# Cross-attention keys and values of two pairs made in the first stage, a causal mask on quarters of the array, expert rows cleared ahead, and a router on unscaled tokens

## The chip, the cores and the metric

One core of one Trainium2 chip. The metric is device microseconds from the start of the program to its end. Three timed runs of the kernel before and one profiled execution are at hand.

## The reference

The input x is 16 tiles of 128 tokens by 256 features in float32, the context likewise. Four blocks run one after another:

1. `q = layernorm(x)`, `x = x + q + tril(C C^T) q` per tile, where C is the tile's context.
2. With `h = layernorm(x)`: a latent attention of 16 heads of 8 features (RMS norm, a projection to 128, rotated queries and keys, causal softmax, projection up), whose result is added to h to give r. Then eight experts of 512 hidden features: `t = rmsnorm(r) * g2`, softmax over `t @ router_w`, the two best experts' `silu(t w1) * (t w3) @ w2`, weighted by their two probabilities normed to 1. `x = x + r + y`.
3. Cross attention of 16 heads of 64 features: queries from a layer norm of x, keys and values `C @ w_kv`, which depend on the context alone. `x = x + tanh(gate) * (out @ w_out + b_out)`.
4. `t = layernorm(x)`, 16 experts of 256 hidden features, the two best by `t @ router_w` with sigmoid weights, and a shared expert of 512. All added to x.

## The kernel before

**Order of work.** Nothing is scheduled at run time. `latent_phases`, `expert_phases`, `cross_phases`, `shared_phases` and `last_phases` (L165 to L380) list phases: an engine, an estimated duration in ns, what the phase comes after, the PSUM banks that it fills and a due time. `Plan.order` (L108) simulates the engines and always takes the phase with the smallest start plus due time; `LEAD` (L76) moves the due time of all phases of a name. What comes out is one fixed order for each engine's queue (TensorE, VectorE, ScalarE, GpSimd and SP, which issues DMAs), and an engine stands still at a phase whose semaphores aren't there yet, whatever is behind it.

**First stage, 16 batches b of one tile each.** `ctx`/`q1` (L668, L679) make block 1; `hnT`, `c`, `qkv` project; GpSimd's `rope_p` (L1756) and VectorE's `rope` rotate; `qkT` transposes queries and keys; `qkh`/`qkl` split them in a high and a low part, and GpSimd's `kmh`/`kml` (L1771) spread the keys over four masked copies, by `masked` (L639). `s(b)` (L713) first writes the causal mask into four banks of 512 columns with four bf16 products of the identity and `negb` (L718), then waits for `kmh` and `kml` and adds three products on groups of 32 array rows (L727). `max`, `exp`, `pT` (L731, transposes at L737), `pT_e` (L1048, a copy out of PSUM at L1052), `pv` (L740, 64 matmuls at L751), `onrm` and `wup` follow; `r` (L1340) makes the residual tile r. Then comes a chain: `sq` (L1054) squares on ScalarE, `eps3` on VectorE, `pow3` on GpSimd, and `tt` (L1358) on VectorE writes `r * rstd * g2` to a token tile TT. `tT` (L761) transposes TT (L765, L766), `log` makes the router's logits, `ra` and `rb` (L1367, L1389) the choice and the row that each token gets, and `sc` (L1789) on GpSimd scatters the token to its expert's rows in the DRAM tensor `xs_dram` (8 or 16 experts of 2176 rows of 259 floats).

**Between first stage and experts.** `route` (L1408) makes the list TI of tiles (expert and first row), 39 at most. An expert's last tile is only partly filled, so `pad_sp` (L1855) and `pad_act` (L1067) write 128 zero rows behind each expert's last, four experts on SP's queue and four on ScalarE's. `xs(0, 0)` (L1866) waits for the list, all scatters, all pads and `latent_over`, reads the row from TI and loads the first 128 rows. `xT` first issues `FILL[0]` = 40 matmuls (`keep_busy`, L784), which compute nothing that is used. `wa`, `wv` copy the expert's weights; `gate_up` (L800, matmuls at L812), `down` (L816, three matmuls on high and low parts by `mm3`, L661 to L665) and `y` do a tile.

**Cross attention, 8 pairs jj of two tiles.** For a pair TensorE makes keys in four units `K(jj, u, half)` (L827, 12 matmuls of 256 columns each, by `mm3`), values in four units `V(jj, u, i)` (L840, 6 of 512 columns), queries `Q` likewise, then `S`, `T`, `PV`, `W`. Keys lie in a ring of three tiles, values in one of seven. `ch`/`cl` split a pair's context, `kw`/`vw` and `kwl`/`vwl` the weights. Blocks of the shared expert (`SG`, `SD`) are spread over the end of this stage and of the last one. `pad_sp(1)` clears the second experts' rows ahead of `xs(1, 0)`.

**Loads.** `loads` (L1843) issues on SP, with no wait: x tiles 0 to 3 (0.5 MB), constants (0.3), context tiles 0 to 3 (0.5), small weights (0.6), x tiles 4 to 15, context tiles 4 to 15 (1.6), the first experts' gate and up weights (8.4 MB) and down weights (4.2).

## Time and profile before

| | us |
|---|---|
| three timed runs | 995.28, 1000.51, 1004.29 |
| median | 1000.51 |
| profiled execution, whole | 990.24 |
| its span | 988.4 |
| mean granted TensorE clock in it | 0.981 |

The profile is of one execution. Its times are from the start of the span. PE is TensorE's matmuls, PEld its weight loads, DVE VectorE, ACT ScalarE, POOL GpSimd, SP SyncE; L12 is line 12 of the kernel. A row of a timeline has start, duration, engine, line, operation, output and inputs, count, and in brackets an idle time before it and what ended it. Matmuls are pipelined, so durations of neighbours overlap; the distance between starts is what one costs.

### The profile page before, as it was taken

The numbers are of one execution on the slowest core, as the hardware profiler recorded it, in microseconds if no ns is written. First come the engines' busy times: TensorE is split into PE (matmuls) and PEld (weight loads), VectorE is DVE, ScalarE is ACT, GpSimd is POOL, SyncE is SP. The second block draws the span as 40 slices with busy tenths as digits, with TensorE's granted clock in tenths as the row PEclk, the third lists the DMA queues.
The fourth block names the chain that finished last, engine by engine and source line by source line (L and its number), as shares of the span: only waits on it lengthen the run. The fifth ranks groups of instructions, "written<-read, shape, count | busy, mean of one in ns | idle before, by whom it ended". The sixth has DMA issues, their size and how long they took to land.

```text
span 988.4 us, 24441 instructions
## 1 busy us (share of the span) xinstructions
PE 911.9 (92%) x8250; PEld 815.2 (82%) x8250; DVE 720.7 (73%) x1957; ACT 609.8 (62%) x1690; POOL 289.3 (29%) x371
## 2 busy tenths in 40 slices
PE   5798888879999999978999999999998999999997
PEld 3566666547999999977988999989887979999986
DVE  6877788664766667666898887566686736888857
ACT  1378777734666666655776686575877425767640
POOL 3747767640000000005645432202011202333320
PEclk9999999979999999988999999999999999999999
DMA  9700000012411111113101010000040872333325
GB/s 378 341 13 18 29 34 24 27 45 78 144 50 54 50 54 49 49 31 125 39 28 55 24 33 23 23 2 23 1 172 22 333 218 72 93 91 98 93 93 212
DMA packets 37323, 82.57 MB, mean 84 GB/s; under 512 B 5489, under 2 KB 28785, under 8 KB 35921
## 3 DMA queue, kind: packets, MB, share of 16 engines
q1 hardware_dynamic: 29760, 61.63, 17.9%
q0 software_dynamic: 6864, 18.85, 5.7%
q8 instruction: 68, 1.11, 0.5%
q10 hardware_dynamic: 576, 0.53, 0.2%
q14 instruction: 55, 0.44, 0.2%
HBM read 55.95 MB, written 25.04 MB: 82 GB/s over the span
## 4 chain that ended last, share of the span: by engine, by line
PE 62%; issue 13%; DVE 9%; POOL 6%; DMA 4%; ACT 3%; SPq 3%; ACTq 0%; DVEq 0%; POOLq 0%
PE ps L812 15%; PE ps L663 9%; PE ps L665 8%; PE ps L664 8%; POOL yt_dram L1820 4%; PE ps L876 4%; PE ps L897 3%; PE ps L886 3%; DVE BIG L1328 2%; PE ps L737 2%; PE ps L727 1%; PE ps L718 1%; DMA CT<-in_ctxT 1%; SPq L1864 1%; PE ps L955 1%
## 5 line engine op out<-in xcount | busy, mean ns | idle before, releaser
L663 PE MATMUL ps<-BIGR 128*128 128x256 f32 (+1 forms) x826 | 258.6, 313 | 12.5 <-DVE CTR L1576 4.7
L812 PE MATMUL ps<-BIG 128*128 128x128 f32 x2000 | 253.0, 276 | 5.9 <-DVE BIG L1556 4.9
L812 PEld LDWEIGHTS ps<-BIG 128*128 128x128 f32 x2000 | 238.5, 193 | 8.2 <-DVE BIG L1556 6.8
L665 PE MATMUL ps<-BIGR 128*128 128x256 f32 x762 | 216.3, 284 | 0.0
L663 PEld LDWEIGHTS ps<-BIGR 128*128 128x128 f32 x826 | 158.4, 192 | 20.2 <-issue 10.4
L664 PE MATMUL ps<-BIGR 128*128 128x256 f32 (+1 forms) x570 | 168.6, 296 | 0.0
L665 PEld LDWEIGHTS ps<-BIGR 128*128 128x128 f32 x762 | 145.7, 191 | 0.0
L1098 ACT COPY BIG<-BIG 128x512 f32 (+1 forms) x86 | 70.0, 814 | 99.4 <-PE ps L812 93.6
L664 PEld LDWEIGHTS ps<-BIGR 128*128 128x128 f32 x570 | 109.1, 191 | 1.8
L1549 DVE TENSOR_TENSOR BIGR<-BIG,BIGR 128x512 fp32r<-128x512 f32 (+1 forms) x86 | 80.3, 934 | 36.4 <-ACT BIGR L1107 36.2
L1812 POOL DMA_INDIRECT BIG<-ys_dram,YI x32 | 36.2, 1131 | 231.5 <-DMA ys_dram<-BIG 223.7
L1192 ACT ACTIVATE BIG<-ps,sm 128x128 f32<-128x128 f32 x256 | 91.6, 387 | 14.8 <-DVE sm L1650 14.6
L1799 POOL DMA_INDIRECT xs_dram<-TT,PI x64 | 65.9, 1030 | 82.3 <-DVE PI L1406 71.3
L1820 POOL DMA_INDIRECT yt_dram<-BIG,IX x47 | 47.7, 1016 | 127.8 <-DVE BIG L1569 124.9
L1045 ACT ACTIVATE BIG<-ps,BIG 128x128 f32<-128x128 f32 x256 | 72.5, 409 | 9.9 <-DVE BIG L1328 9.9
L1734 POOL TENSOR_TENSOR st<-st,CS 128x1 f32<-128x1 f32 (+1 forms) x48 | 31.0, 647 | 160.8 <-DVE st L1277 160.6
L664 PE MATMUL ps<-CTR,BIGR 128*128 128x256 f32 x256 | 73.2, 286 | 0.0
L1556 DVE TENSOR_TENSOR BIG<-ps,BIG 128x256 f32<-128x256 f32 (+1 forms) x86 | 46.7, 543 | 36.2 <-PE ps L812 36.2
L1107 ACT CAST BIGR<-BIG 128x512 fp32r (+1 forms) x86 | 69.4, 807 | 5.4 <-PE ps L665 5.4
L1647 DVE TENSOR_REDUCE sm<-ps 128x4 f32<-128x512 f32 x64 | 44.0, 687 | 25.8 <-PE ps L876 25.6
L1192 ACT ACTIVATION_READ_ACCUMULATOR BIG<-ps,sm 128x1 f32 x256 | 57.5, 225 | 0.0
L1542 DVE COPY BIG<-BIG 128x512 f32 (+1 forms) x86 | 47.2, 549 | 7.8 <-issue 4.0
(224 smaller groups left out, 1905.0 us busy)
## 6 DMA issues: line engine op xcount, KB each, us to landing
BIG<-in_wd SPq DMA_DIRECT2D x2, 4096.0 KB, 35.3
BIG<-in_wgu SPq DMA_DIRECT2D x1, 6144.0 KB, 19.2
BIG<-xs_dram SPq DMA_DIRECT2D x47, 129.5 KB
BIG<-xs_dram SPq DMA_DIRECT2D x39, 128.0 KB
ys_dram<-BIG SPq DMA_DIRECT2D x39, 128.0 KB, 1.7
BIG<-yt_dram SPq DMA_DIRECT2D x16, 256.0 KB, 5.7
xs_dram<-zero SPq DMA_DIRECT2D x20, 129.5 KB, 6.8
X<-in_x SPq DMA_DIRECT2D x4, 512.0 KB, 7.7
```

The lines of the kernel that those rows point to most:

```text
L663: pe.matmul(o, l[0], r[0], start=start, stop=False)
L664: pe.matmul(o, l[0], r[1], start=False, stop=False)
L665: return pe.matmul(o, l[1], r[0], start=False, stop=stop)
L812: i = pe.matmul(o[:, c * 128:(c + 1) * 128], wt[:, at:at + 128], x[:, k * 128:(k + 1) * 128], start=k == 0, stop=k == 1)
L1045: i = act.activation(p_[g][:, at], ps("s", b, i=g)[:, at], ACT.Exp, bias=sm[:, 4 * g + n:4 * g + n + 1])
L1098: act.copy(W_[r][j % 2][:, n:2 * n], WGU[:, bass.ds(e * (2 * n) + n, n)]).then_inc(S["gu_upper"], 1)
L1107: act.copy(D_[j % len(D_)][:, 0:n], WD[:, bass.ds(e * n, n)]).then_inc(S["down_hi"], 1)
L1192: i = act.activation(xp_[s % 4][:, at], ps("S", s // 2, i=s % 2)[:, at], ACT.Exp, bias=sm[:, 4 + n:5 + n], accum_out=sm[:, 8 + n:9 + n])
L1542: v.tensor_copy(W_[r_][j % 2][:, 0:n], WGU[:, bass.ds(e * (2 * n), n)]).then_inc(S["gu_lower"], 1)
L1549: v.tensor_tensor(wd[:, n:2 * n], WD[:, bass.ds(e * n, n)], wd[:, 0:n].bitcast(F32), ALU.subtract).then_inc(S["down_lo"], 1)
L1799: pool.indirect_dma_start(XS, bass.IndirectOffsetOnAxis(ap=PI[:, b, k:k + 1], axis=0), TT[tile_of(r, b)][:, :], None).then_inc(sem(f"scatt ...
L1820: pool.indirect_dma_start(YT, bass.IndirectOffsetOnAxis(ap=IX[:, j % 4:j % 4 + 1], axis=0), Y_[1][j % 3], None).then_inc(sem(f"results_pla ...
```

## The change

1. **Keys and values of pairs 4 and 6** (`EARLY_KV`). The 2.1 MB of `wkv` and the two pairs' contexts are loaded at once after the first four loads (`wkv_in`), ahead of the rest of x and context (`rest_in`). `kvw` on ScalarE and `kvwl` on GpSimd split the weights in four parts, `ctxh`/`ctxl` the contexts. 16 units `kv(m)` on TensorE, of the same matmuls as K and V before, fill a bank of the first stage; `kv_e` copies it to one of four tiles and `kv_s` stores that (0.26 MB) to DRAM. In cross attention `kl` and `vl` load them back in place of the K, V, `K_e` and `V_e` phases of these pairs. The expert weights' region is used for this, so they are loaded in parts: down weights behind `kmh(3)`, a quarter of the gate and up weights behind the four `kvwl`, the other 6.3 MB (`load_w0b`) when all 16 stores have landed.
2. **Mask.** `causal(b)` replaces the four products of 128 by 128 by eight on quarters of 64 by 64 (four of 512 and four of 256 columns), placed between the first and the second of the three products; the first no longer waits for `kml`.
3. **Router.** `tT` transposes r itself instead of TT, the router's weights are scaled by g2 once, the logits' difference is multiplied by rstd in `gates_a`. `r(b)` also waits for `tT(b-2)`.
4. **Rows cleared ahead.** `pad_act` and `pad_sp(0)` go. Seven groups of two and one of three blocks of 128 rows of all eight experts are cleared by SP during the first stage (`blank`), each scatter of batch 2g waits for group g. `xs` reads TI before its waits.
5. `FILL[0]` is 30 instead of 40. `LEAD` has other values throughout, and a new table `NUDGE` moves single phases by up to 4.6 us of due time; so the orders of all engines differ.

```diff
-FILL = (40, 24)
+BLANK = [range(2 * g, 2 * g + 2) for g in range(7)] + [range(14, 17)]
+EARLY_KV = (4, 6)
+FILL = (30, 24)
...
+        due += LEAD.get(...) + NUDGE.get(key, 0)
...
+    p.add("SP", 60, ("wkv_in",), ("loads",), late=12000)
+    p.add("SP", 200, ("rest_in",), ("wkv_in",), late=17000)
+    for g in range(len(BLANK)):
+        p.add("SP", 120, ("blank", g), ("tt", 2 * g - 2) if g else ("kmh", 0), late=4000)
+    p.add("SP", 60, ("wd_in",), ("rest_in",), ("kmh", 3), late=12000)
-        add("PE", 220, ("tT", b), ("tt", b), banks=[(misc, ("tT_e", b))])
+        add("PE", 220, ("tT", b), ("r", b), ("log", b - 2), banks=[(misc, ("tT_e", b))])
+    for u in range(4):
+        p.add("ACT", 950, ("kvw", u), ("setup_a",), ("wkv_in",))
+        p.add("POOL", 2050, ("kvwl", u), ("kvw", u))
+    p.add("SP", 60, ("load_w0a",), ("kvwl", 3), ("kmh", 3), late=12000)
+    for j in range(len(EARLY_KV)):
...
+        for m in range(8 * j, 8 * j + 8):
+            add("PE", 1440, ("kv", m), ("ctxl", j), ("kvwl", ...), ("kv_s", m - 4), banks=[("misc", ("kv_e", m))])
+            add("ACT", 466, ("kv_e", m), ("kv", m), ("kv_s", m - 4))
+            add("SP", 60, ("kv_s", m), ("kv_e", m), late=2000)
+    p.add("SP", 60, ("load_w0b",), ("kv_s", 8 * len(EARLY_KV) - 1), ("load_w0a",), late=18000)
...
                 for x, y in ((0, 0), (0, 1), (1, 0)):
+                    if y:
+                        causal(b)
+                        pe.wait_ge(*done("kml", b))
...
+            def causal(b):
+                for n in range(2):
+                    for half in range(2):
+                        for rows in range(2):
+                            g, at = 2 * (rows ^ half) + n, slice(64 * rows, 64 * rows + 64)
+                            lo = 64 * half
+                            m = (negb if rows == half else negx)[at, lo:128].rearrange("p (o t) -> p o t", o=1)
+                            o = ps("s", b, i=g)[64 * half:64 * half + 64, :].rearrange(...)[:, :, lo:128]
+                            pe.matmul(o, identb[at, at], m.broadcast_to([64, 4, 128 - lo]), start=False, stop=False)
...
             def tT(b):
-                pe.wait_ge(*done("tt", b))
-                tt = TT[tile_of(0, b)]
+                pe.wait_ge(*emptied("wup", b))
+                t = r_[b % 2]
...
+            def kv_e(m):
+                act.wait_ge(*full("kv", m))
+                if m >= 4:
+                    act.wait_ge(sem(f"kv_stored{m % 4}"), 16 * (m // 4))
+                act.copy(kvs_[m % 4], ps("kv", m)[:, :]).then_inc(*frees("kv", m))
...
+            def blank(g):
+                if g:
+                    sp.wait_ge(*done("tt", 2 * g - 2))
...
+                for c in BLANK[g]:
+                    sp.dma_start(XS[0:E0 * CAP, 0:D].rearrange("(e c) n -> c e n", c=CAP)[128 * c:128 * c + 128],
+                                 zero[:, 0:D]...broadcast_to([128, E0, D])).then_inc(sem(f"cleared{g % 3}"), 16)
...
             def xs(r, j):
                 if j == 0:
                     sp.wait_ge(sem("tiles_listed"), r + 1)
+                at = sp.value_load(TI[j:j + 1, 1:2], ...)
+                if j == 0:
                     for i in range(3):
                         sp.wait_ge(sem(f"scattered{i}"), ...)
-                    sp.wait_ge(sem("padded_sp"), 16 * (E1 * r + E0 // 2))
-                    sp.wait_ge(sem("padded_act"), 16 * (E0 // 2))
+                    if r:
+                        sp.wait_ge(sem("padded"), 16 * E1)
...
+            def load_w0b():
+                for i in range(4):
+                    sp.wait_ge(sem(f"kv_stored{i}"), 16 * len(range(i, 8 * len(EARLY_KV), 4)))
+                sp.dma_start(big(0, 48 * KB), a["wgu0"][:, 0:48 * KB]).then_inc(sem("wgu_loaded"), 16)
```

## Rows read from the trace of the kernel before

**Rows 1.** The page's first part: busy us, share of the span, instructions.
```profile
PE 911.9 (92%) x8250; PEld 815.2 (82%) x8250; DVE 720.7 (73%) x1957; ACT 609.8 (62%) x1690; POOL 289.3 (29%) x371
```

**Rows 2.** Stretches: length; busy PE, PEld, DVE, ACT, POOL; clock; DMA; GB/s.
```profile
0.00:46.00 46.00, 26.92 (x138) 18.96 (x138) 34.57 (x135) 12.21 (x45) 26.29 (x55) 0.96 0.94 386
46.00:212.00 166.00, 145.08 (x1820) 105.14 (x1820) 129.13 (x389) 125.62 (x425) 105.04 (x151) 0.98 0.07 24
...
232.00:435.00 203.00, 202.60 (x1771) 202.63 (x1772) 135.51 (x188) 128.34 (x191) 0.00 (x0) 0.99 0.20 60
...
450.00:600.00 150.00, 146.06 (x1277) 131.37 (x1276) 127.25 (x373) 103.27 (x350) 69.10 (x74) 0.99 0.12 37
600.00:757.00 157.00, 153.62 (x1443) 138.94 (x1441) 106.54 (x336) 113.78 (x399) 25.10 (x27) 1.00 0.11 40
757.00:813.00 56.00, 53.86 (x396) 49.18 (x391) 32.16 (x103) 19.01 (x30) 7.15 (x8) 1.00 0.69 244
```

**Rows 3.** TensorE's timeline in cross attention, 461.9 to 467.6 us.
```profile
461.89 0.28 PE L663 MATMUL ps<-BIGR 128*128 128x256 f32 x1
...
464.77 0.40 PE L663 MATMUL ps<-BIGR 128*128 128x512 f32 x1
...
467.34 0.39 PE L665 MATMUL ps<-BIGR,CTR 128*128 128x512 f32 x1
```

**Rows 4.** TensorE's timeline in the first stage, 103 to 115 us.
```profile
103.31 0.97 PE L727 MATMUL ps<-BIGR 32*128 32x512 f32 x12
...
111.93 0.17 PE L781 MATMUL ps<-mb,strictb 128*128 128x8 bf16 x1 [0.88 <-DVE mb L1387]
...
113.02 1.03 PE L718 MATMUL ps<-negb,identb 128*128 128x512 bf16 x4
113.98 0.98 PE L727 MATMUL ps<-BIGR 32*128 32x512 f32 x12
114.89 1.95 PE L751 MATMUL ps<-BIG 128*32 128x128 f32 x64
```

**Rows 5.** Groups by line in 50 to 205 us: busy, mean ns, idle before.
```profile
L765 PE MATMUL ps<-CS,TT 128*128 128x128 f32 x14 | 4.2, 302 | 4.5 <-DVE TT L1361 4.4
...
L1052 ACT COPY BIG<-ps 128x512 f32<-128x512 f32 x60 | 36.8, 623 | 7.3 <-PE ps L737 6.5
...
L641 POOL TENSOR_TENSOR BIGR<-BIGR,CS 128x512 fp32r<-128x512 f32 x26 | 26.8, 1042 | 10.5 <-ACT BIGR L1036 10.4
```

**Rows 6.** Timeline of all engines between the first stage and the experts.
```profile
212.00 0.48 DVE L1346 SCALAR_TENSOR_TENSOR BIG<-BIG,st,ps 128x256 f32<-128x256 f32 x1 [0.85 <-PE ps L759]
...
214.96 0.45 PE L765 MATMUL ps<-CS,TT 128*128 128x128 f32 x1 [1.36 <-DVE TT L1361]
...
218.26 11.26 PE L787 MATMUL ps<-negb,identb 128*128 128x512 bf16 x40
...
220.79 0.96 POOL L1799 DMA_INDIRECT xs_dram<-TT,PI  x1 [0.31 <-issue]
...
223.82 0.15 DVE L1469 CAST TI<-sc 128x1 int32<-128x1 f32 x1
...
226.56 1.04 ACT L1107 CAST BIGR<-BIG 128x1024 fp32r x1
...
229.35 3.71 SPq L1882 DMA_DIRECT2D BIG<-xs_dram  x4
...
232.40 2.74 PE L812 MATMUL ps<-BIG 128*128 128x128 f32 x16 [0.51 <-issue]
```

**Rows 7.** DMA queues in 220 to 229 us, issues in 60 to 200 us.
```profile
q10 hardware_dynamic: 576, 0.53, 23.2%
...
xs_dram<-TT,PI POOLq DMA_INDIRECT x26, 2.7
```

**Rows 8.** The chain that ended last: two waits for DMAs (start, length).
```profile
4.42 12.19 DMA CT<-in_ctxT
...
224.25 4.06 DMA xs_dram<-zero
```

More of the change, by code:

```diff
@@ L28 @@
 VPAD = 88
-FILL = (40, 24)
+EARLY_KV = (4, 6)
+LAST_KV = max(j for j in range(NB // 2) if j not in EARLY_KV)
+FILL = (30, 24)
 KB = 256
@@ L100, in add @@
         name = (engine, key[0], key[1] if key[0] in BY_STAGE else 0)
[L101 removed]
+        due += LEAD.get(key[0] + str(key[1]) if key[0] in BY_STAGE else key[0], 0) + NUDGE.get(key, 0)
         if name in self.latest:
@@ L253, in expert_phases, with ctx_before @@
             add("SP", 60, "ys", ("y", r, j), late=2000)
+def ctx_before(j):
+    return max((i for i in range(j % 2, j, 2) if i not in EARLY_KV), default=-1)
 def cross_phases(p):
@@ L869, in scores @@
                 if i == 0:
-                    pe.wait_ge(*emptied("K", jj, u, 1))
+                    if jj in EARLY_KV:
+                        n = 2 * jj + u
+                        pe.wait_ge(sem(f"keys_back{n % 3}"), 16 * len([x for x in range(n % 3, n + 1, 3) if x // 2 in EARLY_KV]))
+                    else:
+                        pe.wait_ge(*emptied("K", jj, u, 1))
                     pe.wait_ge(*emptied("Q", jj, u, 1))
@@ L892, in PV @@
                 pe.wait_ge(*emptied("T", 2 * h + 1))
-                pe.wait_ge(*emptied("V", jj, u, i))
+                if jj in EARLY_KV:
+                    pe.wait_ge(sem(f"values_back{h % 7}"), 16 * len([x for x in range(h % 7, h + 1, 7) if x // 4 in EARLY_KV]))
+                else:
+                    pe.wait_ge(*emptied("V", jj, u, i))
                 v = xv_[h % 7]
@@ L1000, in setup @@
                 act.copy(negb[:, :], cst["neg"]).then_inc(sem("constants_cast"), 1)
+                for x in range(2):
+                    act.copy(negx[64 * x:64 * x + 64, :], cst["neg"][64 - 64 * x:128 - 64 * x, :]).then_inc(sem("constants_cast"), 1)
                 act.wait_ge(sem("small0_loaded"), 16)
@@ L1004, in setup @@
                 act.mul(wqkv[:, 0:128], wqkv[:, 0:128], SC0).then_inc(sem("w_down_scaled"), 1)
+                for k in range(2):
+                    act.mul(rt0[:, k, :], rt0[:, k, :], g2c[:, k:k + 1]).then_inc(sem("router_scaled"), 1)
             def hnT_e(b):
@@ L1790, in sc @@
                 pool.wait_ge(*done("rb", r, b))
-                if r == 0 and b == 0:
-                    pool.wait_ge(sem("zeroed"), 6)
+                if r == 0:
+                    pool.wait_ge(*done("tt", b))
+                    if b == 0:
+                        pool.wait_ge(sem("zeroed"), 7)
+                    for g in range(len(BLANK)):
+                        if BLANK[g][0] == b:
+                            pool.wait_ge(sem(f"cleared{g % 3}"), 16 * sum(len(BLANK[k]) for k in range(g % 3, g + 1, 3)))
                 if r and b == 0:
```

297 lines of the change are left out of this document (219 added, 78 removed), and 78 rows, old and new, of tables (LEAD, NUDGE).

## The prediction

> **What bounds the kernel now.** I read the engines' busy shares first. TensorE is busy 92% of the span, VectorE 73%, ScalarE 62%, GpSimd 29% [rows 1], so I asked where its idle 76.5 us lie. The table by stretches answers that [rows 2]. In the experts' first pass (232 to 435 us) TensorE is idle 0.4 of 203 us; in cross attention (450 to 757) 7.3 of 307; up to 813 another 2.1 of 56. Work taken from there comes off the time nearly one for one. The first stage (0 to 212) is different: 19.1 us idle in its first 46, then 20.9 of 166, while VectorE and ScalarE are busy 129 and 126 us of those 166. A batch takes 10.67 us there (103.31 to 113.98, products of batch to batch [rows 4]), and TensorE's own work 87% of that: it is the bound here as well, but with holes, 0.88 us in front of the count at 111.93 for instance [rows 4]. Then comes a tail without much matmul: from the last residual (212.00) to the first expert's gate product (232.40) there are 20.4 us [rows 6].
>
> The sum is made against the profiled execution: 988.4 us of span and 1.8 us around it, 990.2. The three timed runs have a median of 1000.5, which is 10.3 more; I take the same 10.3 for the kernel after.
>
> **Keys and values of pairs 4 and 6.** They leave cross attention and are made in the first stage. A K unit is 12 matmuls of 256 columns: two units run from 461.89 to 464.77, so 1.44 us each. A V unit is 6 of 512 columns: two from 464.77 to about 467.57, 1.40 each [rows 3]. A pair has 4 and 4: 11.4 us, and two pairs 22.7 us. TensorE gives this up where it is 98% busy. I take 21.0: VectorE is the next engine there, busy 106.5 of the 157 us of 600 to 757, which hold some four pairs (307 us for 8, 38.4 each), so 26 us a pair, while TensorE is left with 27 in pair 4 or 6 [rows 2]. It is close, and rings of three key tiles let neighbours even it out, so only 1.7 us are left behind. The bounds are 12 us (VectorE rules in both pairs) and 22.7. The four loads of keys and eight of values that replace the units go over SP, which has almost nothing else there, each a ring slot ahead of its use; they cost nothing unless SP stands at a wait for something later.
>
> **The same work in the first stage** adds 22.7 us to TensorE. ScalarE gets 16 copies like the 623 ns ones [rows 5] (10.0), four roundings of 1024 weight columns (1.04 us each by the nearest row, at 226.56 [rows 6]) and two context ones, 15 us in all; VectorE 1.4 us. GpSimd gets four subtractions of 1024 columns, twice the 512 of its 1042 ns row [rows 5]: 8.3 us, and they come in the first 46 us, where it is busy 26.3 [rows 2]. They can delay the first batches by up to 5 us, but these are the very holes in which the new matmuls lie. How much of 22.7 is hidden? Nothing at least; at most 15, half of the 19 us idle at the start and a third of the 21 later, since most of those later holes are shorter than a unit of 1.4 us. The weights can't be ready before some 20 us: with what is queued in front of them they are 4.5 MB, 12 us at the 386 GB/s of the first 46 us [rows 2], and rounding and subtraction follow. So I take 7.0, nearer the low end. The two later loads of the context and X move behind the new weights; batch 4 waits for the context until 16.6 us already [rows 8], and I count a shift of 2 us inside the same 7.0.
>
> **Mask.** Four matmuls of 512 columns lie from 113.02 to 113.98, 0.96 us [rows 4]. Now eight act on quarters of 64 by 64: four of 512 and four of 256 columns. If the quarters run side by side this is two of 512, 0.43 us; one after another it is 6 of 512, 1.28. The nearest rows are the products on 32 rows of the array: 12 of 512 columns in 0.91 us (113.98 to 114.89), against 4 whole ones in 0.96 [rows 4]. Those pack, so I take side by side. Twelve such products would be 0.64 us if four run together without loss, and they take 0.91: entering a packing has a price of 0.1 to 0.25. I take 0.66 for the mask, a gain of 0.30 a batch and 4.8 us in 16 batches; bounds 8 gained and 5 lost. The Trainium skill (TensorEngine Tiling (Array Packing), Key Properties) says that changing the tiling mode drains the array; after this edit the mode changes twice more in each batch. The 0.27 us that the 12 products take over 0.64 agree with a cost of that kind; no run here yet shows it alone. By the page's other rule, tiles that run independently, the gain without drains would be 8 us.
>
> **Router on unscaled tokens.** The transposes no longer wait for the square sum, the power and the scaling: 14 pairs of them start right after the scaling and wait 4.5 us on it [rows 5]. I take 2.5, since the next thing in TensorE's order then waits for its own input. At the end it counts whole: the last transposes start at 214.96 and could at 212.62, 0.14 behind the end of the residual (212.00 + 0.48): 2.3 us [rows 6].
>
> **Rows cleared ahead.** Between the tile list (223.82 + 0.15) and the first row load (229.35) stand eight DMAs of zeros, which land at 228.31 [rows 6, 8]. They go; what is late next is the last scatter (issued from 220.79 on, 2.3 earlier by the router's step, landing 2.7 later [rows 6, 7]) and the tile list at about 221.6. A load issued at 222.5 gives a gate product 3.05 later (229.35 to 232.40), at 225.5: 6.9 us sooner, of which 2.3 are the router's. I round both to 7.0. The filling matmuls, 30 instead of 40, at 0.28 each (11.26/40 [rows 6]) end at about 224.3 and don't hold it up. In exchange 17 blocks of 8 x 128 rows of 1 KB are cleared under the first stage: 17,408 packets. The pads of ScalarE's queue took 23.2% of 16 engines' time over 9 us (220 to 229) for 576 packets, 58 ns each [rows 7], so 17,408 take 63 us of the DMAs in a stage that uses 7% of them [rows 2]. A group of two blocks holds SP's queue 7.4 us, every 21.3 us. The first experts' weights now come late: 6.3 MB, 16.3 us at 386 GB/s, issued when the last K/V store has landed; needed at 222, so they are hidden if the last unit is made before 200.
>
> **Sum.** Cross attention -21.0; first stage +22.7 - 4.8 - 2.5 - 7.0 = +8.4; tail -7.0. Together -19.6. The reordered queues elsewhere (the table of leads) I count as 0, bounds 4 either way. 990.2 - 19.6 = 970.6, as a median of runs 980.9: **981 us**.
>
> **Rivals.**
> A. The first stage absorbs nothing, and GpSimd's 8.3 us delay its start by 4: +7.0 + 4.0, 992. For it: GpSimd and VectorE are both busy in 17 to 46 us. Against: TensorE's 19 idle us there. Chance 0.12.
> B. Better packing: 14 us absorbed and the whole 22.7 in cross attention: 8.7 less, 972. For it: K/V units depend on nothing of a batch and can stand in any hole. Chance 0.20.
> C. VectorE or the rings rule in pairs 4 and 6; only 12 of 22.7 come back: 990. For it: 26 against 27 us above. Chance 0.10.
> D. The clearing paces the first stage: the scatter of batch 2g waits for group g, issued two batches before, and K/V stores and the late weights stand behind it in SP's queue. The price is the packet's time: a group fits its 21.3 us up to 166 ns a packet, 2.9 times the 58. At 225 ns a group takes 28.8, 7.5 too long; over 7 intervals 52.5 us, less the slack of one group (21): +31, 1012, slower. Against it only the 58 ns, measured on 129 KB pieces in another stretch. Chance 0.08. On order the Trainium skill (DMA: Bandwidth & Descriptors, HWDGE ordering) says that one issuing engine's descriptors are taken in ring order on each DMA engine. By that a K/V store waits out at most one group; no run here shows it. By rows that is 7.4 us, and with four store tiles a copy waits only if units follow closer than about 2 us.
>
> **Numbers.** Forecast 0.50 (974 to 988), B 0.20, A 0.12, C 0.10, D 0.08. A median moves by about 1% without a cause, so 990.5 is the border of faster. Faster: the forecast, B, and most of C, 0.80. Same: A and the rest of C, 0.12. Slower, over 1010.5: D, 0.08. The range leaves out half of B and D: 968 to 996.
>
> **What would show it.** Right: experts' first gate product between 230 and 238; nine or ten K/V units before 100 us; a mask step of 0.6 to 0.7 us between its neighbours; row load within 1 us of the tile list; cross attention (first K to last W) 19 to 22 us shorter with TensorE still over 97%. Wrong: batches over 11.5 us apart, ScalarE waiting for stores or VectorE for scatters (D), a mask step over 0.96, a wait for the experts' weights behind the tile list, or VectorE over 95% busy in pairs 4 and 6 (C).

## The result, and the profile after

Over 20 runs each the kernel after takes 992.3 us in the median (986.5 to 997.5), the kernel before 999.7 (993.1 to 1004.5). The ratio is 0.9931 [0.9912, 0.9951]: 7.3 us less in the medians, where 19.6 were forecast. On two more chips it was 0.9943 [0.9908, 0.9978] and 0.9982 [0.9946, 1.0017]. The profiled executions say the opposite, 990.2 before and 996.3 after, because single executions differ by 10 us and chips by 15 (medians of before from 985 to 1000). So the sizes below come from ratios, and the profiles only say where the time lies. Both kernels were profiled again with the experiments (c2_before, c1_after and c4_after below). The first row is a start in us from the start of the span, the others are the lengths of the stages behind it:

```
                              before  before   after   after   after
                              first   again    first   again   third
last residual of first stage  212.0   218.8    227.2   225.7   218.7
  to first gate product        20.4    21.4     22.1    23.6    23.8
first experts                 210.1   209.2    209.2   209.7   209.5
cross attention, to the
  second gate product         374.9   377.3    352.9   353.2   352.9
second experts                135.1   130.5    145.5   138.0   139.8
rest                           35.9    35.7     37.6    37.6    37.6
```

(Experts: first gate product to last result copy in the first, to last gate product in the second.) Cross attention gives 22 to 24 us, as forecast. But the tail behind the last residual is 2 us longer instead of 7 shorter, and the second experts, whose arithmetic the change doesn't touch, take 8 us more in the mean (141.1 against 132.8).

The page's busy times of after, which answer to [rows 1]:

```profile
PE 909.2 (91%) x8304; PEld 810.8 (82%) x8304; DVE 724.2 (73%) x1957; ACT 610.3 (61%) x1694; POOL 294.7 (30%) x375
```

TensorE's work is 2.7 us less than before, its idle time 9 us more. The stretches of after, columns as in [rows 2]: first stage, tail, first experts, cross attention from the first scores to the last output, and on to the second gate product:

```profile
46.00:227.00 181.00, 160.47 (x1999) 117.34 (x1997) 136.63 (x422) 132.12 (x443) 114.75 (x170) 0.98 0.53 158
227.00:249.00 22.00, 11.01 (x42) 4.96 (x42) 10.95 (x49) 4.17 (x8) 5.20 (x6) 0.68 0.84 328
249.00:452.00 203.00, 202.71 (x1774) 202.69 (x1775) 136.61 (x192) 128.36 (x191) 0.00 (x0) 0.99 0.20 61
483.00:759.00 276.00, 264.20 (x2504) 236.24 (x2503) 227.33 (x694) 193.76 (x713) 85.85 (x95) 1.00 0.17 55
759.00:811.00 52.00, 51.28 (x356) 46.14 (x355) 27.44 (x91) 15.61 (x25) 4.67 (x5) 1.00 0.73 262
```

The second row is the tail: TensorE half idle, the DMA engines 84% busy, where the forecast had a nearly silent tail. What they move stands on SP's queue (start, time of the group, tile, count) and in the chain:

```profile
205.43 3.67 SPq L2180 DMA_DIRECT2D kv_dram<-BIG  x2
209.15 2.73 SPq L2123 DMA_DIRECT2D xs_dram<-zero  x3
213.22 3.71 SPq L2180 DMA_DIRECT2D kv_dram<-BIG  x2
226.57 0.33 SPq L2186 DMA_DIRECT2D BIG<-in_wgu  x1
245.94 7.42 SPq L2154 DMA_DIRECT2D BIG<-xs_dram  x5
```
```profile
233.65 12.11 DMA xs_dram<-TT,PI
245.94 2.10 DMA BIG<-xs_dram
```

in the landing of the weights' load (source L2186), and in the waits of 226 to 252 us:

```profile
DMA to landing us min/median/max: 18.4/18.4/18.4
```

```profile
ACT BIG L1308 <- DMA BIG<-in_wgu: 13.6, 1, 13.6
PE ps L984 <- DMA BIG<-xs_dram: 8.6, 1, 8.6
```

The tile list is ready at 236.4, as forecast about 9 us behind the last residual; the row load is issued at 245.94. In between it waits for the last scatter, which lands after 12.11 us, at 245.8, instead of after 2.7 [rows 7]. The 6.3 MB of first-expert weights run at the same time: issued at 226.57, because the last stores of keys and values, issued from 213 to 217, land only then, and landed 18.4 us later, at 245.0. ScalarE's copy of the first expert's weights (L1308) waits 13.6 us for them and ends at 247.0. So the gate product of 249.3 stands behind both, and a last scatter that landed sooner would by itself have won about 2 us (an estimate from these two times). The ScalarE copies of the 16 units show when these were made:

```profile
L1357 ACT COPY BIG<-ps x16: 567/598/740, 22.9 to 214.1; 128x512 f32<-128x512 f32 x16
```

Eight of them are done by 46 us, hidden in the start; the other eight come only from 164 us on, at the end of the plan. The forecast had written "hidden if the last unit is made before 200".

### The profile page after: what moved, and what is told of

Its sections match the earlier page's. It is cut to its first block, busy times and chain, and to the rows that moved or that the text cites. A ratio compares the mean times of both kernels' runs of the same rounds, so it can differ in the third digit from the quotient of the medians.

```text
span 994.5 us, 24561 instructions
## 1 busy us (share of the span) xinstructions
PE 909.2 (91%) x8304; PEld 810.8 (82%) x8304; DVE 724.2 (73%) x1957; ACT 610.3 (61%) x1694; POOL 294.7 (30%) x375
## 3 DMA queue, kind: packets, MB, share of 16 engines
q8 instruction: 68, 1.11, 0.5%
## 4 chain that ended last, share of the span: by engine, by line
PE 55%; issue 15%; DVE 14%; POOL 5%; ACT 5%; DMA 4%; another core or an unknown queue 0%; SPq 0%; DVEq 0%; POOLq 0%; ACTq 0%
PE ps L999 15%; PE ps L833 7%; PE ps L835 7%; PE ps L834 7%; POOL yt_dram L2066 4%; ACT BIG L1262 3%; PE ps L1086 2%; PE ps L1110 2%; PE ps L1096 2%; PE ps L921 2%; PE ps L897 2%; PE ps L1168 2%; DVE BIG L1884 1%; PE ps L935 1%; DMA xs_dram<-TT,PI 1%
## 5 line engine op out<-in xcount | busy, mean ns | idle before, releaser
L833 PE MATMUL ps<-BIGR 128*128 128x256 f32 (+1 forms) x826 | 260.4, 315 | 12.2 <-DVE BIGR L1807 3.3
L835 PE MATMUL ps<-BIGR 128*128 128x256 f32 x778 | 223.1, 287 | 0.0
L834 PE MATMUL ps<-BIGR 128*128 128x256 f32 (+1 forms) x602 | 179.0, 297 | 0.0
L833 PEld LDWEIGHTS ps<-BIGR 128*128 128x128 f32 x826 | 159.1, 193 | 20.3 <-issue 14.2
L835 PEld LDWEIGHTS ps<-BIGR 128*128 128x128 f32 x778 | 149.2, 192 | 0.7
L1308 ACT COPY BIG<-BIG 128x512 f32 (+1 forms) x86 | 70.1, 815 | 108.5 <-PE ps L999 70.0
L834 PEld LDWEIGHTS ps<-BIGR 128*128 128x128 f32 x602 | 116.3, 193 | 1.8
L1420 ACT ACTIVATE BIG<-ps,BIG 128x128 f32<-128x128 f32 x256 | 91.2, 384 | 15.6 <-DVE BIG L1887 12.8
L2066 POOL DMA_INDIRECT yt_dram<-BIG,IX x47 | 45.6, 971 | 143.0 <-DVE BIG L1800 140.3
L1262 ACT ACTIVATE BIG<-ps,BIG 128x128 f32<-128x128 f32 x256 | 72.6, 394 | 3.1 <-DVE BIG L1557 2.5
L834 PE MATMUL ps<-CTR,BIGR 128*128 128x256 f32 x224 | 63.6, 284 | 0.0
L1335 ACT CAST BIGR<-BIG 128x256 fp32r<-128x256 f32 (+1 forms) x86 | 43.0, 500 | 23.5 <-DVE BIG L1787 22.1
L1420 ACT ACTIVATION_READ_ACCUMULATOR BIG<-ps,BIG 128x1 f32 x256 | 56.8, 222 | 0.0
L1773 DVE COPY BIG<-BIG 128x512 f32 (+1 forms) x86 | 46.8, 544 | 13.5 <-issue 11.2
## 6 DMA issues: line engine op xcount, KB each, us to landing
BIG<-xs_dram SPq DMA_DIRECT2D x47, 129.5 KB
```

Of the source, the lines that this page charges most:

```text
L833: pe.matmul(o, l[0], r[0], start=start, stop=False)
L834: pe.matmul(o, l[0], r[1], start=False, stop=False)
L835: return pe.matmul(o, l[1], r[0], start=False, stop=stop)
L1262: i = act.activation(p_[g][:, at], ps("s", b, i=g)[:, at], ACT.Exp, bias=sm[:, 4 * g + n:4 * g + n + 1])
L1308: act.copy(W_[r][j % 2][:, n:2 * n], WGU[:, bass.ds(e * (2 * n) + n, n)]).then_inc(S["gu_upper"], 1)
L1420: i = act.activation(xp_[s % 4][:, at], ps("S", s // 2, i=s % 2)[:, at], ACT.Exp, bias=sm[:, 4 + n:5 + n], accum_out=sm[:, 8 + n:9 + n])
```

## The experiments

Labels c1 to c5 are five chips; all runs of one number share a chip and its runs of before. "Control" is the kernel after on the same chip; c2, c3 and c5 have none. A figure in brackets behind a ratio is its 95% interval.

**Repeats.** Both kernels again, for the table above.

> The changed kernel again, unchanged, for a second profile beside the first and a second ratio. If the profile of after is typical of it: last r about 227, first gate product of the first experts 20 to 23 us behind it, last wx about 759, and the second experts (first gate product to last) about 145 us. If the 10.4 us that the second experts took longer than in before were chance, this profile has them near 135 instead. Ratio 0.990 to 0.996.

Measured: 0.9943 [0.9908, 0.9978].

> The kernel before again, for a second profile. If the first profile was typical: last r at 212, first gate product at 232, last wx at 769, the second experts about 135 us. Its first profile (990.2 us) lies below all 20 timed runs, so I expect some stage to be 5 to 10 us longer here, most likely one with many waits for DMAs.

Measured: 0.9996 [0.9963, 1.0028]. The stage that differed was the first, by 6.8 us in the last residual; it is spread over the batches, of which some take 12.0 instead of 10.7 us. The second experts came out shorter, not longer.

> After unchanged, as the control on this chip: last r to first gate product 22 to 24 us, second experts 135 to 146 us, ratio 0.992 to 0.996.

Measured: 0.9982 [0.9946, 1.0017].

**The late units.** Orders of three engines edited behind the planner, the eight late units all made before 182 us; the banks of their outputs chosen anew:

```diff
+MOVED = [("PE", ("kv", 15), ("pT1", 11)), ..., ("ACT", ("kv_e", 15), ("exp0", 12)), ...,
+         ("SP", ("kv_s", 15), ("load_w0b",)), ("SP", ("load_w0b",), ("blank", 6)),
...
+    for engine, key, ahead_of in MOVED:
+        orders[engine].insert(orders[engine].index(ahead_of), key)
```

> Units 8 to 15 of the early keys and values moved from batches 9 to 13 to batches 1 to 9 in the orders of TensorE, ScalarE and SP; nothing else. Theory T1, the last stores hold back the load of the 6.3 MB of expert weights, and this load shares the rings with the last scatters: the load is issued before 205 instead of at 226.6 and has landed before the first row load, the last scatter lands in under 6 us instead of 12.1, and the first gate product follows the last r by 13 to 16 us instead of 22.1; the total falls by 3 to 8 us against after (some of it given back because the first stage packs worse, r 15 up to 5 us later), ratio to before 0.983 to 0.990. Rival T2, the weights were ready about when the rows were anyway and the tail is the chain over the last batch: the distance from r 15 to the gate product stays over 20 us and the total does not fall, ratio 0.993 or above. Rival T4, the loss is all in the first stage, which cannot hide the units wherever they stand: as T2, with r 15 at 227 or later.

Measured: 0.9894 [0.9817, 0.9971], 4 runs. The weights were issued at 183.9, the tail fell to 14.0 us; the control had 23.6. But the last residual came at 235.2 instead of 225.7, so the first gate product stood at 249.2 as before. T1 is right about the tail, and its gain was lost again in front of it. Of the 9.5 us, 4.6 are there by the residual of batch 12 (199.8 against 195.1), over the batches that took the units in. For the rest, the stretches of c1_kv_sooner show one cause:

```profile
190.00:195.00 5.00, 4.99 (x92) 3.43 (x84) 2.11 (x4) 3.80 (x14) 4.05 (x4) 1.00 1.03 436
195.00:200.00 5.00, 3.00 (x12) 1.92 (x12) 2.84 (x9) 2.81 (x10) 2.19 (x4) 0.69 1.02 363
200.00:205.00 5.00, 4.32 (x26) 2.13 (x27) 2.14 (x9) 0.93 (x5) 0.73 (x1) 0.50 0.79 244
205.00:210.00 5.00, 4.45 (x64) 3.85 (x66) 3.24 (x10) 4.33 (x15) 2.08 (x2) 0.50 0.92 220
```

The third figure from the right is the granted clock. With no units left there TensorE stood idle for 1.4 us ahead of 188.5 and for 1.7 ahead of 196.7, and the clock went from 1.00 to 0.50, from 2.4 to 1.2 GHz, until about 210. (A second one has no name: ScalarE waits 6.7 us, until 232.5, for something that the profile doesn't tell.) The next experiment puts fill products there:

```diff
                 vacant(pe, *key)
+                keep_busy(ps(*key), {(1, 12): 5, (3, 13): 6, (1, 13): 6}.get((g, b), 0))
```

> The kernel with units 8 to 15 moved ahead, with 17 fill products (0.21 us each at full clock) on TensorE at the three places of batches 12 and 13 where it waited 1.4 to 1.7 us for ScalarE or VectorE. Its first stage was 9.5 us longer than that of after, of which 4.7 behind r 12, where no unit is left, and the granted clock was 0.50 to 0.69 from 195 to 210. Theory: the units at the end of the stage kept TensorE busy enough for the full clock; with fill in their place the clock is 0.94 or above in 195 to 210, r 15 comes 3 to 6 us sooner (229 to 232) and the first gate product at 243 to 246 instead of 249.2. Rival: the clock does not fall for idle time in this place, or r 12 to r 15 is set by the expert weights loading at that time beside the scatters: r 15 stays at 235.

Measured: 0.9895 [0.9858, 0.9931]; last residual at 225.5, gate product at 238.9. Beside a control:

> The units moved ahead with fill at the three idle places, again, beside the control on one chip. From the pairs so far (0.9895 against 0.9931 to 0.9943): 3 to 5 us below the control in the median; first gate product 8 to 10 us sooner in the profile. If the total falls by as much as the gate product is sooner, 8 us or more; if less, the rest goes into the second experts again, which took 144.8 in its first profile.

Measured: 0.9906 [0.9864, 0.9947], median 975.5 against 983.6 of the control. Gate product 240.1 against 242.5, second experts 137.1 against 139.8. The same stretches of c4_sooner_fill:

```profile
195.00:200.00 5.00, 4.29 (x35) 2.06 (x34) 2.80 (x10) 2.42 (x10) 1.81 (x4) 1.00 0.79 251
200.00:205.00 5.00, 4.27 (x80) 3.46 (x80) 4.45 (x18) 4.67 (x16) 2.06 (x3) 1.00 1.09 283
205.00:210.00 5.00, 3.23 (x30) 1.78 (x30) 2.88 (x6) 2.59 (x9) 3.54 (x5) 1.00 0.98 234
```

Seventeen products that compute nothing kept the clock at 1.00, with the DMA engines as full as without, and the step from residual 12 to 13 is 11.2 us instead of 14.7 (the controls have 11.6 and 12.1). The tail is 13.9 us instead of 23.8, but the last residual comes 7.5 us later than in the control, and this lateness (8.2 us) is there by the residual of batch 12: units at the end of the stage are hidden better than units in its middle, and what the early load wins in the tail is mostly paid for with that. The two spans differ by 8.8 us: 2.4 up to the first gate product, which is what the edit did, 3.7 from there to the second, 2.7 in the second experts. The last two parts I can't put down to the edit.

**The load in two.**

```diff
             def load_w0b():
+                sp.wait_ge(*full("kv", 8 * len(EARLY_KV) - 1))
+                sp.dma_start(big(0, 32 * KB), ...)
                 for i in range(4):
                     sp.wait_ge(sem(f"kv_stored{i}"), ...)
-                sp.dma_start(big(0, 48 * KB), ...)
+                sp.dma_start(big(32, 16 * KB), ...)
```

> After with the 6.3 MB load in two: 4.2 MB as soon as the last unit of keys and values is made (no wait for its stores), 2.1 MB behind the stores. If the wait for the stores is what costs: first part issued at 216 to 217 instead of 226.5, gate product 3 to 6 us sooner. If the rings are full anyway until 224 with the clearing writes, the bytes only queue up sooner: gate product sooner by under 2 us, and the last scatters land later than in after. I hold the second likelier.

Measured: 0.9923 [0.9885, 0.9961], tail 20.9 us. The first part was issued at 208.4, 11 us ahead of the second, and the second landed at 236.3, 16.8 us behind its own issue, with the last scatter at 237.3. The ratio can't be told from that of after (0.9931). A wait less was worth at most 3 us of tail here, while the rings (the DMA engines' queues) were full: the clearing writes, the first part and the scatters share them.

**The clearing writes.** One batch sooner (and the last two groups each ahead of a store in SP's order), then all of them early:

```diff
-                    sp.wait_ge(*done("tt", 2 * g - 2))
+                    sp.wait_ge(*done("tt", max(2 * g - 3, 0)))
```

> The clearing writes of groups 1 to 7 are paced one batch earlier (wait for tt 2g-3 instead of 2g-2), and in SP's order group 6 stands ahead of the store of unit 9 and group 7 ahead of that of unit 12. Theory T3, the last stores of keys and values queue behind the three writes of group 7 (issued at 209.15) and land late, and the weights with them: the load of the weights is issued by 221 instead of 226.6, the first gate product comes 3 to 6 us sooner after r 15, ratio 0.988 to 0.991. T1 without this queueing (the stores are late because the units are made late): under 2 us. Rival D of the prediction, clearing itself slows the stage: no change either, since as much is written.

Measured: 1.0003 [0.9965, 1.0041]. It did not test what it was made for: the last group was issued at 206.90 instead of 208.13, since the scaling it now waited for is done only then. It is somewhat slower than the control for a reason that I did not find.

```diff
+CLEAR = [range(0, 2), range(2, 6), range(6, 17)]
-                    sp.wait_ge(*done("tt", 2 * g - 2))
+                    sp.wait_ge(*done("tt", g - 1))
-                for c in BLANK[g]:
+                for c in CLEAR[g]:
```

> After with the same 17 clearing writes in three groups instead of eight (2, 4 and 11 blocks, paced by tt 0 and tt 1, in SP's order where groups 0 to 2 stood), so that the last ends near 140 us and none stands behind 180. Theory: in after the three writes of the last group (issued at 209, 3.1 MB) keep the rings at 250 GB/s and full until about 224, the last two stores of keys and values and the last scatters land behind them, and the load of the expert weights can start only at 226.5. Then here: the load is issued at 216 to 219, the row load at 236 to 240 instead of 246, the first gate product 5 to 10 us sooner than the 249.3 of both profiles of after, ratio 0.984 to 0.989. Rival, the same bytes written in a burst from 85 to 135 us delay the scatters there and with them the rows of three batches: the first stage to r 8 grows by 3 us or more and eats it. Rival, the load of 6.3 MB alone sets the tail: gate product sooner by less than 3 us.

Measured: 1.0113 [1.0050, 1.0176], slower than before. The rings between 80 and 140 us, the scatters in that stretch, and a wait of GpSimd in 151 to 175:

```profile
80.00:140.00 60.00, 50.30 (x643) 36.55 (x642) 47.68 (x155) 43.86 (x151) 40.52 (x62) 1.00 1.08 275
```
```profile
xs_dram<-TT,PI POOLq DMA_INDIRECT x10, 8.8
```
```profile
POOL xs_dram L2048 <- DMA xs_dram<-zero: 12.1, 1, 12.1
```

The scatters landed after 8.8 us in the median instead of 2.7, one waited 12.1 us for the clearing of its rows, and one batch took 21.1 us (8 to 9, against 11.8 to 13.4 in the profiles of after). This is the mechanism of rival D, at a place where I had put it myself.

> Both edits on after: clearing early and the load in two. Rings are free from 216 on: first part issued at 216, all weights landed by 234 to 236, gate product at 237 to 242 (after: 249.3), total 8 to 12 us below after, ratio 0.981 to 0.986. If the tail is not set by these loads: as after, 0.993.

Measured: 1.0018 [0.9986, 1.0050], the same stall. The tail is 17.0 us, which neither edit alone reached (23.2 and 20.9), but the gate product stands at 247.7, not at 237 to 242.

**The small parts.** In the kernel before, without early keys and values and with its own order. Clearing rows ahead brings along the edit of `xs`, so c2_three and c2_clear read a tile's row address ahead of the waits as after does; c2_mask does not. The router's part has no run of its own.

> Before with the three small parts alone: mask in quarters, router on unscaled tokens, rows cleared ahead (with 30 instead of 40 fill products); no early keys and values, the order of before. By the terms of the prediction (4.8 mask, 2.5 router wait, 7.0 tail): total 10 to 14 us below before, ratio 0.986 to 0.990, so that the small parts are worth more than the whole change and the early keys and values cost 3 to 7. Rival T4, the small parts are hidden by the chain of a batch: under 4 us, ratio over 0.996, and then the early keys and values bring all the gain.

Measured: 0.9975 [0.9938, 1.0011].

> Before with only the rows cleared ahead in place of the padding writes at the end, and 30 fill products. Prediction: no zeros between the last scatter and the row load, first gate product 5 to 7 us nearer to the last r (13.4 to 15.4 instead of 20.4), first stage not longer, ratio 0.993 to 0.995. Rival D, clearing 17 blocks of 2048 rows loads the DMA rings and the scatters: r 15 at 216 or later, or the last scatter over 6 us, and a ratio of 0.998 or above.

Measured: 1.0016 [0.9965, 1.0066]. Its profile has the tail at 15.9 us instead of 21.4, the padding writes gone as forecast, and the total does not fall: the second experts take 138.0 us against 130.5 in c2_before, and 140.7 in c2_three. That pointed to the last pair of experiments.

> Before with only the mask made on quarters of the array. Prediction: 0.30 us per batch off TensorE, 3 to 5 us off the first stage, ratio 0.995 to 0.997. Rival, the whole products lay in a wait for kmh and kml and cost nothing: ratio 0.999 to 1.002.

Measured: 0.9996 [0.9951, 1.0042]. And the mask undone in after (four whole products ahead of the wait, as in before):

> After with the mask put back as four whole products per batch ahead of the wait for kmh, 16 batches. Theory of the prediction (quarters save 0.30 us of TensorE per batch and TensorE paces the stage): r 15 comes 4 to 6 us later and the total is 4 to 6 us above after, ratio 0.997 to 1.000. Rival, the quarters save TensorE time but put their products behind the waits, where the whole products lay in front of them in an idle stretch: the total stays within 2 us of after. The other way, the order table was made for the short mask, so more than 6 us.

Measured: 0.9985 [0.9950, 1.0020]; above the control by 2.0 us in the medians, by 4.2 by the ratios. Neither run tells 3 us from none. What the trace says is below.

**The address read.** One edit that I had weighed only for the first row load: SP's read of a tile's row address moved ahead of the waits, for every row load of both groups of experts. Here it goes back behind them for the second group:

```diff
             def xs(r, j):
...
-                at = sp.value_load(TI[j:j + 1, 1:2], ...)
+                if not r:
+                    at = sp.value_load(TI[j:j + 1, 1:2], ...)
...
+                if r:
+                    at = sp.value_load(TI[j:j + 1, 1:2], ...)
                 sp.dma_start(XS_[r][j % 3], ...)
```

> After with one statement moved back: in the second experts SP reads the row's address from the tile list behind its waits, as in before, not ahead of them. The second experts (first gate product to last) took 130.5, 135.1 and 136.4 us in the three profiles with the padding writes and 135 to 147, 140 in the mean, in ten with the clearing writes, and VectorE waited there for scatters of results for 4 to 15 us against 15 to 31. Theory V: the earlier address read lets the row loads start sooner and meet the scatters of results. Then here: the waits for scatters back under 15 us, second experts at or under 136, total 3 to 6 us below the control. Rival: the difference is chance or comes from elsewhere: no change against the control, within 2 us.

Measured: 0.9875 [0.9823, 0.9926], 6 runs, median 974.2 against 983.6 of the control. The two profiles agree to 1 us at every boundary up to the second gate product (804.9 and 804.7); then the second experts take 130.3 us instead of 139.8. VectorE's waits in them (waited for, us, times, longest), and the scatters of results with their median landing, first the control:

```profile
DVE PL L1733 <- DMA yt_dram<-BIG,IX: 23.1, 19, 2.8
```
```profile
yt_dram<-BIG,IX POOLq DMA_INDIRECT x45, 3.0
```

then c4_read_late:

```profile
DVE PL L1733 <- DMA yt_dram<-BIG,IX: 9.8, 12, 1.7
```
```profile
yt_dram<-BIG,IX POOLq DMA_INDIRECT x45, 2.5
```

One tile of the timeline of either, first the control, shows the place of the load (SPq) between the scatters (POOL):

```profile
863.12 0.96 POOL L2066 DMA_INDIRECT yt_dram<-BIG,IX  x1 [1.54 <-DVE BIG L1800]
...
863.61 0.16 DVE L1736 SCALAR_TENSOR_TENSOR IX<-BIG,PL 128x1 int32<-128x1 f32 x1
863.98 0.33 SPq L2154 DMA_DIRECT2D BIG<-xs_dram  x1
```
```profile
861.89 0.96 POOL L2066 DMA_INDIRECT yt_dram<-BIG,IX  x1 [0.35 <-DVE BIG L1800]
...
863.59 0.16 DVE L1736 SCALAR_TENSOR_TENSOR IX<-BIG,PL 128x1 int32<-128x1 f32 x1
...
864.55 2.67 SPq L2157 DMA_DIRECT2D BIG<-xs_dram  x2
...
865.70 0.96 POOL L2066 DMA_INDIRECT yt_dram<-BIG,IX  x1 [2.85 <-DVE BIG L1800]
```

The load waits for IX in both. With the address at hand it goes out 0.2 us behind it (863.77 to 863.98), onto the scatter just issued; with the address still to be read, 0.8 us behind (863.75 to 864.55), when the scatter of 861.89 is over (2.5 us to landing in the median) and the next is 1.2 us away. The index of a tile waits for a scatter four tiles back, and so does everything that VectorE has queued behind it.

That the tile shown is typical can be counted. In c4_after 24 of the 47 scatters have a row load issued less than 0.9 us behind them, in c4_read_late one. The control's trace tells the landing of 16: the eight with such a load behind them took 2.8 to 4.9 us (median 3.25), the other eight 2.4 to 3.2 (median 2.5). In c4_sooner_fill it is 3.6 for 15 with a load and 2.4 for 16 without.

Then the same statement moved alone in the kernel before:

> Before with that one statement moved the other way, as the change moved it: SP reads the row's address ahead of its waits, in both groups of experts; nothing else. Theory V: the row loads are issued 0.2 us behind the release instead of 0.8, meet the scatters of results, the second experts take 137 to 144 us instead of 130 to 136, VectorE waits over 18 us for scatters, the tail behind r 15 is 0 to 1 us shorter; total 4 to 9 us above before, ratio 1.004 to 1.009. Rival: the late read helps only beside the clearing writes or the order of after: ratio 0.998 to 1.002.

Measured: 1.0079 [1.0041, 1.0116], slower; second experts 137.2 us. And the three small parts with the read left where it was:

> Before with the three small parts (mask, router, rows cleared ahead) and the address read for the second experts behind the waits as in before. With the early read these three measured 0.9975. Theory V: 5 to 9 us below that, ratio 0.988 to 0.993, second experts 130 to 136 us, so that the small parts are worth 7 to 12 us of the 14.3 forecast. Rival: the three parts gain little on their own and the early read cost them nothing: 0.996 to 0.999.

Measured: 0.9886 [0.9832, 0.9941], 6 runs; second experts 128.2 us. VectorE's waits in the second experts, first c5_read_early, then c5_three_read_late:

```profile
DVE PL L1505 <- DMA yt_dram<-BIG,IX: 21.3, 19, 1.8
```
```profile
DVE PL L1530 <- DMA yt_dram<-BIG,IX: 2.5, 2, 1.3
```

Theory V holds both ways: taken out of after it gives 9.4 us back, put into before it costs 7.9 (0.79% of 999). Over all 20 profiles the second experts take 128.2 to 136.4 us in the six with the read behind the waits (mean 132.5) and 135.1 to 146.6 in the fourteen with it ahead of them (mean 139.5). The runs show that the place of the read decides. That a load close behind a scatter makes it land later is shown by the landings above; how much of the 8 to 9 us this accounts for is not.

**Units ahead with fill, and the read put back.**

> The last two together: if both hold, 8 to 12 us below the control, ratio to before 0.981 to 0.986; if only the first, as c4_sooner_fill within 2 us.

Measured: 0.9808 [0.9763, 0.9854], 6 runs, median 967.9 us: 17.2 below before on the same chip, 15.7 below after. It beats both kernels, and by about what had been forecast for the change; but it gets there another way, so that is no support for the forecast. In its tail the chain now runs over TensorE's 30 filling products, which compute nothing and end at about 239, just behind the landing of the first rows: a still earlier load alone would win nothing more.

## Why the prediction was wrong

**The number.** 992.3 lies in the range stated, 968 to 996, and where rival A (992) and C (990) had put it. Neither's mechanism was there: the first stage did absorb units, and cross attention gave back 22 us. That it lies in the range is luck; the change was forecast at -19.6 and came out at -7.3.

**The sum.** Forecast -19.6: small parts -14.3 (mask 4.8, router 2.5, tail 7.0), keys and values -5.3 (-21.0 + 22.7 - 7.0), order tables 0. Measured by ratios:

```
                                   forecast   measured
three small parts                    -14.3    -11.4 [-16.8, -5.9]  c5_three_read_late
early keys and values, new order      -5.3    -1 +-7 (0.9875 against 0.9886, two chips)
address read ahead of the waits          0    +7.9 [+4.1, +11.6]   c5_read_early
                                              +9.4 (medians)       c4_after, c4_read_late
all                                  -19.6    -6.9 [-8.8, -4.9]    medians: -7.3
```

The measured rows add up to about -4, with errors of 4 to 7 each. So the ratios show what the address read costs; that the keys and values brought less than 5.3 they don't show, and the profiles have to say where it went. By stages two steps failed, of about the same size.

**The step without a term.** The sum counts the second experts at nothing, without a reason. The nearest that it has is "The reordered queues elsewhere (the table of leads) I count as 0, bounds 4 either way", and the moved address read is not in that table. I had used it, unsaid, for "row load within 1 us of the tile list", where it helps once; it also moved for the 47 row loads of the second experts and costs 8 to 9 us there, more than the 4 that I allowed for everything unnamed. That is about two thirds of the 12 us missed. That row loads and scatters of results share the DMA engines there, and that VectorE waits for these scatters (13.0 us in the first profile of before, 4.3 in the second), was in the traces of before; I had asked only whether an earlier load can hurt the engine that waits for it, not what it runs into.

**The tail, -7.0: measured +2 in the profiles of after. The small parts alone do give the 7.** c5_three_read_late and c2_three have 14.7 and 15.3 us from the last residual to the gate product, against 21.4 of before: 6 to 7 us, as forecast, and the padding writes are gone. In after the late weights take their place. "They are hidden if the last unit is made before 200" named the condition but not the answer: the last unit is made at 214. I had taken "nine or ten units before 100 us"; it was eight, and the planner left the rest for the end. c1_kv_sooner and the kernels with fill show 13.4 to 14.0 us when the load is early, though not for nothing: the last residual then comes 7.5 to 9.5 us later than in their controls. The row load came 9.5 us behind the tile list (236.4 to 245.9), where within 1 us had been the sign. I had ranked the late load as a remark in the clearing's paragraph; it should have been a rival with a price: 18 us of load and the store's landing, less the 12 us of tail.

**First stage, +8.4:** right in size, in part by luck. The last residual is 8.5 us later in the mean of the profiles (227.2, 225.7, 218.7 against 212.0, 218.8), but single pairs give 0 to 15. The eight early units cost almost nothing: the first residual stands at 59.1 to 59.5 in the profiles of after, at 56.9 and 59.5 in those of before. That is 9 us or more of their 11.4 hidden in the start, where I took 7.0 for all 16. Rival B's mechanism was right for these eight. The other eight are hidden well only at the end of the stage, where they hold back the weights: the stage's +8.4 and the tail's loss are one thing, and the sum took the good half of each.

**Router, -2.5 and 2.3 of the tail:** the wait on the scaling (4.4 us in before) no longer appears in front of the transposes in after. What that is worth in time has no run.

**Cross attention, -21.0:** right; 22.0 and 24.1 us by the pairs of profiles. TensorE is 96% busy there (264.2 of 276 us), not over 97%, and VectorE 82%. Rival C, by which only 12 us come back, is out. Up to the last output of the stage it is even 26 and 28 us, more than the 22.7 of work moved out and than the sign of 19 to 22; the stretch behind it, to the second gate product, is 4 longer. Both must come from the new order.

**Mask, -0.30 a batch:** the eight quarter products take less than forecast, but the scores around them more. TensorE's timeline of a batch in after:

```profile
141.80 0.51 PE L897 MATMUL ps<-BIGR 32*128 32x512 f32 x4
142.24 0.40 PE L913 MATMUL ps<-negb,identb 64*64 64x512 bf16 x1
...
142.78 0.73 PE L897 MATMUL ps<-BIGR 32*128 32x512 f32 x8
143.45 0.33 PE L861 MATMUL ps<-CS,BIG 128*128 128x128 f32 x1
```

The mask is 0.54 us (142.24 to 142.78) against 0.96 [rows 4], and the twelve score products, now 4 and 8, take 0.44 + 0.67 = 1.11 against 0.91. Net 0.22 us a batch, 3.5 in all; forecast 0.30, 4.8. The same twelve products take 0.90 in one go in c1_full_mask too, so the 0.20 more comes from splitting them around the mask: two more changes of the tiling mode, by estimate 0.1 us each if they are all of it. The Trainium skill (TensorEngine Tiling (Array Packing), Key Properties) says that a change of the tiling mode drains the array, which fits; no run has the change of mode alone. The mask's weight in the total stays open: both runs on it are within their intervals of nothing.

**Clearing, 63 us of the DMAs:** the total was nearly right (71 us for 17.8 MB at the 250 GB/s of 100 to 140 us in c3_clear_first). Rival D's stall did not come in after: its batches are 7.3 to 13.8 us apart. What I had missed is that, at the end of the stage, the last three blocks, the last stores, the scatters and the weights meet on the same rings. SP's queue alone (packets, MB, share of 16 engines) from 210 to 225 us of after:

```profile
q1 hardware_dynamic: 3457, 3.75, 96.4%
```

The Trainium skill (DMA: Bandwidth & Descriptors, Queues, rings and completion order) says that a DMA engine takes turns between queues packet by packet. The trace agrees only in part. A scatter issued at 229.78, 3.2 us behind the 6.3 MB of another queue, lands at 240.6, 4.4 us ahead of that load; but the last three, issued from 231.1 to 233.7, land at 245.2 to 245.8, just behind the load (245.0). In c1_after and c4_after the last ones land within 1.1 us of the load as well. Taking turns alone doesn't explain that, and these traces don't show what does.

**What stays open.** How much the new order tables cost or give; the last stage and the stretch behind cross attention, 1.8 and 4 us longer in the profiles with them (the 4 are paid back in front, the 1.8 are not); and why c1_blank_sooner was slower than its control.

## What to carry to other kernels

Read a diff for statements that change place inside a wait's shadow, not only for those that change work: here one register read, moved ahead of its waits, cost most of what three real improvements brought. An issue that comes sooner is a gain only if the transfer meets nothing; for each such move list what is on the rings in the next few microseconds. And when work is moved to where it "fits", ask what is freed by its last piece and who waits for that: a condition such as "before 200 us" has to be checked against the order that the planner really writes, or it belongs among the rivals with its full price. A forecast by terms needs a term, if only a range, for every stage that the diff touches.

## What the runs showed of the hardware

- A row load of 129.5 KB issued less than 0.9 us behind a scatter, while that is in flight, goes with a landing of 3.25 us in the median, where the others take 2.5 (c4_after; 3.6 against 2.4 in c4_sooner_fill). In c4_after 24 of 47 scatters are met so, in c4_read_late one, and its second experts are 9.5 us shorter.
- In c1_kv_sooner TensorE was granted the half clock (1.2 GHz) for about 13 us, from 197 to 210, after idle gaps of 1.4 us (ahead of 188.5) and 1.7 us (ahead of 196.7); 17 fill products in three gaps kept it at 1.00 (c3_sooner_fill, c4_sooner_fill). In the kernel after, where the late units stand there, it was 0.83 from 190 to 200 us and 1.00 from there to 225.
- Zeros written in rows of 1 KB fill all 16 DMA engines at about 250 GB/s (100 to 140 us of c3_clear_first), where the weights' load reaches 485 (230 to 235 us of c1_after); beside them scatters land after 8.8 us instead of 2.7.
- The last scatters beside a 6.3 MB load landed within 1.1 us of it, 12 to 15 us after their issue, in all three profiles of after.
- The same kernel differs by 14 us between chips (medians of before 985.2, 989.9, 996.3, 997.4, 999.0).
